# The attention's context product: five bfloat16/float16 products on a block diagonal, or float32 on 32x32 tiles

## The reference, cut to what matters

```
x = x + fake_quant(layernorm(x)) @ fake_quant(ctx)                 # ctx: 16 x 512 x 512
h = layernorm(x)
q, k, v = h @ wq.T + bq, h @ wk.T + bk, h @ wv.T + bv              # reshaped to (token, 32 heads, 16)
scores  = einsum('bshd,bstd->bsht', q, k) / 4                      # heads against heads, for each token
probs   = softmax(scores)
x = x + einsum('bsht,bstd->bshd', probs, v)                        # the context product
x = x + ffn(layernorm(x))     # a router picks 16 of 64 experts of rank 8: z = h @ A.T, times gate, @ B.T
```

## Time and profile before

| | |
|---|---|
| median of 3 runs | 202.35 us (202.15 to 202.36) |
| span of the profiled execution | 198.7 us, 3999 instructions; its own total time is not listed apart from the three runs |
| around the span, against the median | 3.65 us |
| busy: PE / PE weight load / DVE / ACT / POOL | 136.4 / 88.6 / 152.5 / 93.6 / 95.1 us |
| mean granted TensorE clock | 0.887 of 2.4 GHz |
| tiles: q product of tiles 1, 2, 3 starts at | 70.30, 108.81, 144.91 us |

### The profile page before, as it was taken

The page is one execution under the profiler, slowest core; times in us unless marked ns, Lnnn a source line. Parts: engine busy times, 40 slices in busy tenths (PEclk is TensorE's granted clock), DMA queues, the critical chain, the costliest instruction groups (busy, mean ns, idle before and its releaser), DMA issues.

```text
span 198.7 us, 3999 instructions
## 1 busy us (share of the span) xinstructions
PE 136.4 (69%) x1630; PEld 88.6 (45%) x1630; DVE 152.5 (77%) x258; ACT 93.6 (47%) x117; POOL 95.1 (48%) x101
## 2 busy tenths in 40 slices
PE   0012587940904799787957998597799949589884
PEld 0002473410803654336646443393754418585543
DVE  0768579999699657799997679999844999958331
ACT  0289414875892084822693856327016734301120
POOL 2738036668870858753049698313347832201000
PEclk9999999995585579997888999969699996969999
DMA  4999999995738138000000100000010000000101
GB/s 103 422 412 404 398 406 416 372 409 208 269 157 351 76 66 358 3 0 0 3 3 0 52 2 3 0 3 0 3 56 0 0 0 3 0 3 0 54 3 53
DMA packets 7218, 25.20 MB, mean 127 GB/s; under 512 B 1184, under 2 KB 1440, under 8 KB 5280
## 3 DMA queue, kind: packets, MB, share of 16 engines
q1 hardware_dynamic: 7056, 24.94, 32.7%
q10 hardware_dynamic: 144, 0.00, 0.0%
HBM read 23.89 MB, written 1.05 MB: 126 GB/s over the span
## 4 chain that ended last, share of the span: by engine, by line
DVE 53%; PE 17%; issue 12%; POOL 9%; ACT 4%; DMA 2%; POOLq 0%; DVEq 0%; ACTq 0%
PE ps_b L1098 6%; DVE qdiag L756 5%; DVE vdiag L787 4%; DVE vdiag_lo L798 4%; DVE kT L764 4%; DVE qT L743 4%; DVE h L636 3%; POOL q_sb L358 3%; DVE stats L630 3%; DVE probs L636 2%; POOL rstd L343 2%; DMA sc_in<-in_quant_dram 2%; DVE s_max L805 2%; DVE kT_lo L768 2%; DVE vdiag L929 2%
## 5 line engine op out<-in xcount | busy, mean ns | idle before, releaser
L466 ACT ACTIVATE cu<-raw,sc_in,sc_recip 128x2048 uint8<-128x2048 f32 x15 | 30.7, 2085 | 0.8 <-DMA raw<-in_ctx_dram 0.8
L1171 PE MATMUL ps_att<-qT,vdiag 128*128 128x32 f16 x128 | 17.3, 186 | 9.7 <-DVE qT L821 9.7
L352 POOL TENSOR_SCALAR cbf<-cu 128x2048 bf16<-128x2048 uint8 x10 | 19.7, 1974 | 4.8 <-ACT cu L466 4.5
L340 POOL TENSOR_SCALAR var_eps<-mean_var 128x1 f32<-128x1 f32 x12 | 3.6, 301 | 36.0 <-DVE mean_var L632 35.8
L1152 PE MATMUL ps_att<-kT,qdiag 128*128 128x32 bf16 x128 | 10.4, 183 | 14.6 <-DVE kT_lo L768 7.6
L378 POOL TENSOR_TENSOR k_pack<-probs,k_pack 128x512 f16<-128x512 f32 x7 | 9.4, 1351 | 19.0 <-ACT k_pack L535 19.0
L1152 PEld LDWEIGHTS ps_att<-kT,qdiag 128*128 128x128 bf16 x128 | 10.1, 101 | 17.8 <-issue 17.8
L1171 PEld LDWEIGHTS ps_att<-qT,vdiag 128*128 128x128 bf16 x128 | 13.2, 103 | 10.6 <-DVE vdiag_lo L798 10.6
L1172 PE MATMUL ps_att<-qT,vdiag 128*128 128x32 f16 x128 | 17.3, 186 | 0.0
L1173 PE MATMUL ps_att<-qT,vdiag 128*128 128x32 f16 x128 | 17.3, 186 | 0.0
L1174 PE MATMUL ps_att<-qT,vdiag 128*128 128x32 f16 x128 | 17.3, 186 | 0.0
(11 more groups left out here) (141 smaller groups left out, 460.7 us busy)
## 6 DMA issues: line engine op xcount, KB each, us to landing
raw<-in_ctx_dram SPq DMA_DIRECT2D x15, 1024.0 KB, 7.0
raw<-in_ctx_dram SPq DMA_DIRECT2D x2, 512.0 KB, 11.8
wq<-in_L_attn_wq_dram SPq DMA_DIRECT2D x1, 1024.0 KB, 14.1
wk<-in_L_attn_wk_dram SPq DMA_DIRECT2D x1, 1024.0 KB, 10.8
wv<-in_L_attn_wv_dram SPq DMA_DIRECT2D x1, 1024.0 KB, 15.0
wa<-in_L_ffn_A_w_dram SPq DMA_DIRECT2D x1, 1024.0 KB, 18.6
wb<-in_L_ffn_B_w_dram SPq DMA_DIRECT2D x1, 1024.0 KB, 16.1
x_sb<-in_x_dram SPq DMA_DIRECT2D x1, 768.0 KB, 8.6
```

What stands on the lines that cost most here:

```text
L352: nc.gpsimd.tensor_scalar(cbf[:, n % BF_SLOTS, :, :], cu8[:, n % U8_SLOTS, :], -CENTER, 1.0, ALU.add, ALU.mult).then_inc(sem_ctx_bf_pool, 1)
L466: nc.scalar.activation(cu8[:, n % U8_SLOTS, :], raw[:, n % RAW_SLOTS, :], ACT.Identity, bias=sc_in[:, 3:4], scale=sc_recip[:, 2:3]).then_i ...
L1171: nc.tensor.matmul(ps_att[:, i, :], v_hi, e_hi, start=True, stop=False)
```

## The change

The context product takes its two operands as they are, in float32. For each step i PE takes four products, one for each sequence j: the stationary operand is eT (32 partitions of quarter j, 32 columns), the moving one vT (the same partitions, 16 columns and one of ones), and the output 32x17 at the partitions of quarter j. The splitting of v and of the exponentials goes, and with it hi_v, mid_v, the POOL commands for them, place_v, spread_v_lo, both block diagonals with their clearing, and the scaling by 16384. transpose_v takes v_sb and writes vT. transpose_context reads 17 columns a step in place of 32, and oT lies with the channel outside and the head inside. eT, vT, oT, attn, q1 and h1 get buffers of their own, and the waits follow: bias_k waits for k's low part of the tile before in place of x2_ready, bias_v for vT, transpose_q for place_q of the tile before, transpose_probs for the context of the tile before. Scores, order of work, CUT and the filler products stay.

```
@@ buffers @@
-        vdiag = sb("vdiag", [P, Q * P * 2], BF16)
-        vdiag_lo = sb("vdiag_lo", [P, Q * P], BF16)
+        eT = sb("eT", [P, Q, H])
+        vT = sb("vT", [P, Q, HD + 1])
-        e_pack = k_pack[:, :].bitcast(F16)
-        eT = qT[:, :].bitcast(F16)
-        oT = probs
+        oT = sb("oT", [P, HD + 1, H])
-        vT = words(k_sb)
-        attn = k_sb
+        attn = sb("attn", [P, D])
...
@@ gpsimd @@
-            def make_e_lo(t, part):
...
-            nc.gpsimd.memset(words(vdiag_lo), 0).then_inc(sem_v_lo_zeros, 1)
+            nc.gpsimd.memset(vT[:, :, HD:HD + 1], 1.0).then_inc(sem_v_ones, 1)
...
-                take_hi(t + 1, v_sb[:, :], view(v_pack[:, :], 0, [[2, D]]), sem_v_hi, sem_v_rest)
-                make_lo(t + 1, v_sb[:, :], view(v_pack[:, :], 1, [[2, D]]), v_lo[:, :], sem_v_rest, sem_v_mid, sem_v_lo)
-                for part in range(2 if t < TILES - 1 else 1):
-                    make_e_lo(t, part)
...
@@ scalar @@
-            def hi_v(t):
-            def mid_v(t):
...
                 nc.scalar.activation(probs[:, half, :], probs[:, half, :], ACT.Exp,
                                      scale=HD ** -0.5).then_inc(sem_s_exp, 1)
-                act.wait_ge(sem_s_exp, 2 * t + part + 1)
-                act.wait_ge(sem_kT_ready, 2 * (t + 1))
-                nc.scalar.activation(probs[:, half, :], probs[:, half, :], ACT.Copy,
-                                     scale=E_SCALE).then_inc(sem_e_scaled, 1)
-                act.wait_ge(sem_e_scaled, 2 * t + part + 1)
-                nc.scalar.copy(e_pack.rearrange("p (i h w) -> p i h w", h=H, w=2)[:, half, :, 0],
-                               probs[:, half, :]).then_inc(sem_e_hi, 1)
@@ vector @@
             def bias_k(t):
                 if t >= 1:
-                    dve.wait_ge(sem_x2_ready, t)
+                    dve.wait_ge(sem_k_lo, 2 * t)
...
             def transpose_v(t):
-                dve.wait_ge(sem_v_mid, t + 1)
-                dve.wait_ge(sem_k_lo, 2 * (t + 1))
-                nc.vector.transpose(vT.rearrange("p (i d) -> p d i", d=HD),
-                                    words(v_pack).rearrange("p (h d) -> p d h", d=HD)).then_inc(sem_vT_ready, 1)
-            def place_v(t):
-            def spread_v_lo(t):
+                if t == 0:
+                    dve.wait_ge(sem_v_ones, 1)
+                if t >= 1:
+                    dve.wait_ge(sem_context_done, t)
+                dve.wait_ge(sem_v_biased, t + 1)
+                nc.vector.transpose(vT[:, :, 0:HD].rearrange("p i d -> p d i"),
+                                    v_sb[:, :].rearrange("p (h d) -> p d h", d=HD)).then_inc(sem_vT_ready, 1)
...
             def transpose_probs(t, part):
-                nc.vector.transpose(words(qT)[:, values], words(k_pack)[:, values]).then_inc(sem_eT_ready, 1)
+                half = slice(S * part, S * (part + 1))
+                dve.wait_ge(sem_s_exp, 2 * t + part + 1)
+                if t >= 1:
+                    dve.wait_ge(sem_context_done, t)
+                nc.vector.transpose(eT[:, half, :], probs[:, half, :]).then_inc(sem_eT_ready, 1)
...
             def transpose_context(t):
-                nc.vector.transpose(oT[:, :, :], view(ps_att[:, 0, :], 0, [[1, H], [H, Q]])).then_inc(sem_oT_ready, 1)
+                nc.vector.transpose(oT[:, :, :], view(ps_att[:, 0, :], 0, [[1, HD + 1], [H, Q]])).then_inc(sem_oT_ready, 1)
...
-            nc.vector.memset(words(vdiag), 0).then_inc(sem_v_zeros, 1)
...
@@ tensor @@
             def context(t, first, end):
                 if first == 0:
-                    pe.wait_ge(sem_v_diag, 2 * BPT * (t + 1))
-                e_halves = eT.rearrange("p (i h w) -> p i h w", h=H, w=2)
+                    pe.wait_ge(sem_vT_ready, t + 1)
                 for i in range(first, end):
                     if i % S == 0:
                         pe.wait_ge(sem_eT_ready, 2 * t + i // S + 1)
-                    e_hi, e_lo = e_halves[:, i, :, 0], e_halves[:, i, :, 1]
-                    v_hi = view(vdiag[:, :], 2 * P * i, [[2, P]])
-                    v_mid = view(vdiag[:, :], 2 * P * i + 1, [[2, P]])
-                    nc.tensor.matmul(ps_att[:, i, :], v_hi, e_hi, start=True, stop=False)
-                    nc.tensor.matmul(ps_att[:, i, :], v_hi, e_lo, start=False, stop=False)
-                    nc.tensor.matmul(ps_att[:, i, :], v_mid, e_hi, start=False, stop=False)
-                    nc.tensor.matmul(ps_att[:, i, :], v_mid, e_lo, start=False, stop=False)
-                    last = nc.tensor.matmul(ps_att[:, i, :], vdiag_lo[:, P * i:P * (i + 1)], e_hi, start=False,
-                                            stop=True)
+                    for j in range(BPT):
+                        rows = slice(Q * j, Q * (j + 1))
+                        last = nc.tensor.matmul(ps_att[rows, i, 0:HD + 1], eT[rows, i, :], vT[rows, i, :],
+                                                start=True, stop=True)
```

More of the change, by code:

```diff
@@ L250, in build @@
         zgT = sb("zgT", [P, KC, P])
[L252 to L254 removed]
+        q1 = sb("q1", [P, 2, D], BF16)
+        h1 = sb("h1", [P, 2, D])
         ps1 = ps("ps1", [P, 2, 512])
@@ L371, in finish_norm_3 @@
                                         ALU.mult, ALU.mult).then_inc(sem_ln3_shift, 1)
-            def make_e_lo(t, part):
[L375 to L379, removed]
             def residual_2(t):
                 pool.wait_ge(sem_o_recip, t + 1)
-                pool.wait_ge(sem_v_diag, 2 * BPT * (t + 1))
-                nc.gpsimd.tensor_tensor(attn[:, :].rearrange("p (h d) -> p h d", d=HD), oT[:, :, 0:HD],
+                nc.gpsimd.tensor_tensor(attn[:, :].rearrange("p (h d) -> p h d", d=HD),
+                                        oT[:, 0:HD, :].rearrange("p d h -> p h d"),
                                         view(o_recip[:, :], 0, [[1, H], [0, HD]]), ALU.mult).then_inc(sem_o_scaled, 1)
@@ L512, in mid_k @@
                         .then_inc(sem_k_mid, 1)
-            def hi_v(t):
-                act.wait_ge(sem_v_biased, t + 1)
-                if t >= 1:
-                    act.wait_ge(sem_v_diag, 2 * BPT * t)
-                nc.scalar.copy(view(v_pack[:, :], 0, [[2, D]]), v_sb[:, :]).then_inc(sem_v_hi, 1)
-            def mid_v(t):
-                act.wait_ge(sem_v_rest, t + 1)
-                nc.scalar.copy(view(v_pack[:, :], 1, [[2, D]]), v_sb[:, :]).then_inc(sem_v_mid, 1)
             def exp_scores(t, part):
@@ L771, in transpose_v @@
             def transpose_v(t):
-                dve.wait_ge(sem_v_mid, t + 1)
-                dve.wait_ge(sem_k_lo, 2 * (t + 1))
-                nc.vector.transpose(vT.rearrange("p (i d) -> p d i", d=HD),
-                                    words(v_pack).rearrange("p (h d) -> p d h", d=HD)).then_inc(sem_vT_ready, 1)
-            def place_v(t):
-                dve.wait_ge(sem_vT_ready, t + 1)
                 if t == 0:
-                    dve.wait_ge(sem_v_ones, BPT)
+                    dve.wait_ge(sem_v_ones, 1)
                 if t >= 1:
                     dve.wait_ge(sem_context_done, t)
-                for j in range(BPT):
-                    rows = slice(Q * j, Q * j + Q)
-                    nc.vector.tensor_copy(
-                        words(vdiag).rearrange("p (i m) -> p i m", m=P)[rows, :, Q * j:Q * j + HD],
-                        vT.rearrange("p (i d) -> p i d", d=HD)[rows]).then_inc(sem_v_diag, 1)
-            def spread_v_lo(t):
-                if t == 0:
-                    dve.wait_ge(sem_v_lo_zeros, 1)
-                dve.wait_ge(sem_v_lo, t + 1)
-                for j in range(BPT):
-                    rows = slice(Q * j, Q * j + Q)
-                    nc.vector.transpose(
-                        words(vdiag_lo).rearrange("p (i m) -> p m i", m=P // 2)[rows, Q * j // 2:(Q * j + HD) // 2, :],
-                        words(v_lo).rearrange("p (h d) -> p d h", d=HD // 2)[rows]).then_inc(sem_v_diag, 1)
+                dve.wait_ge(sem_v_biased, t + 1)
+                nc.vector.transpose(vT[:, :, 0:HD].rearrange("p i d -> p d i"),
+                                    v_sb[:, :].rearrange("p (h d) -> p d h", d=HD)).then_inc(sem_vT_ready, 1)
             def softmax_shift(t, part):
@@ L928, in _ @@
             copy_q1T(0)
-            nc.vector.memset(words(vdiag), 0).then_inc(sem_v_zeros, 1)
-            dve.wait_ge(sem_v_zeros, 1)
-            for j in range(BPT):
-                nc.vector.memset(view(vdiag[Q * j:Q * j + Q, :], 2 * (Q * j + HD), [[2 * P, Q]]), 1.0)\
-                    .then_inc(sem_v_ones, 1)
             center_ctx(2)
```

42 lines of the change are left out of this document (8 added, 34 removed).

## The result

| | before | after |
|---|---|---|
| median (range, 4 runs each) | 202.25 us (199.48 to 202.36) | 193.3 us (191.53 to 195.1) |
| profiled execution: time, span, mean granted clock | span 198.7, 0.887 | 193.27, span 191.5, 0.902 |
| q product of tiles 1, 2, 3 starts at | 70.30, 108.81, 144.91 | 64.56, 102.18, 137.62 |
| DVE's transpose of the last context product | 178.77 | 170.33 |

The account below looks back on a forecast made before the run. VectorE was taken to bound the kernel (busy 77%, 53% of the last chain). Tiles 0 to 3 gave -1.7 + 3.7 + 5.3 + 4.0 = +11.3; span 198.7 became 210.0, plus 3.65 gave 213.7 us, range 195 to 227.

Parts of the forecast that it names:

- 45 ns a pair: Context products on PE: each pair of weight load and matmul costs 45 ns, with load and stream not overlapping.
- the first rival: Context products on PE: weight loads hidden behind streams, 30 ns a pair, 198.3 us; chance 0.27.
- the rule quoted in the prediction: PE's context products: a weight load overlaps multiplies in flight only where the row group differs.
- my sum of +11.3: Whole kernel: tiles 0 to 3 change by -1.7, +3.7, +5.3 and +4.0 us, together +11.3.
- The second rival: Context products on PE: a token's four matmuls overlap fully, 84 ns a token, DVE's h2 binds, 184 us; chance 0.07.
- Four at a time: Context products on PE: four matmuls of a token run at once, 2.7 us a tile, 184 us; chance 0.07.
- cbf at 17.81: Prologue on DVE: without clearing vdiag, the centring of context 2 starts at 17.6 instead of 18.80.
- The third rival: PE's clock stays low with small tiles: a pair averages 55 ns or more, +21.5, so 224 us; chance 0.25.
- My lower end for a pair: Context products on PE: with the load hidden and only issue spacing counting, a pair costs 26 ns.
- The fourth case: Context products on PE: a token's four matmuls overlap fully and cost one matmul, 84 ns; 184 us, chance 0.07.
- the case without overlap: Context products on PE: loads and streams in sequence, 45 ns a pair (38 to 50), 206 to 219 us; chance 0.37.

Follow-up runs that it names:

- the combined version: Changed kernel with the late context load, four fillers ahead of the last context product, nine between its halves, four and four in tiles 1 and 2's gaps: 185.0 us.

## Why the prediction was wrong

**The step that failed** is "In the new loop every matmul uses another part of the array. With nothing hidden [...] I add 3 for part of that gap and take **45 ns a pair**". Measured: 8.5 ns at the high clock, 13.5 at the low. Two errors in one. The row of the router shows a gap between a product on 16 rows and one on the full array; I read it as a rule for moving between parts. Among four equal tiles it is the reverse: a move to another tile is what lets the work overlap, 26 ns when it never moves for eight tokens, 13.7 with two tiles, 8.5 with four. And even in one tile loads are hidden at the high clock: 26 is about the 27 of the load that the first rival had, not the 42 of load and stream in sequence, so the rule quoted in the prediction, by which such a pair would never overlap, did not hold here. 45 is only seen at the low clock, and that it is my number is chance. (8.5 - 45) ns x 1.02 us a nanosecond is -37 us, which would turn my sum of +11.3 into -26; -7.2 came. The rest was never on the path, since PE then waits. A smaller term failed beside it: I had let the q product of tile 1 run at the high clock, 0.7 us less, and it took 5.69 in place of 4.42.

**The second rival had it**, "Four at a time", with a chance of 0.07: its sign, spacing under 15 ns, and VectorE's h2 as what is late next. Its 184 was 9 us too fast, and here are its steps, measured:

- Tile 0: h2 ready at 60.7, forecast and measured. But q at 64.56, not 62.0: the standstill and the load before it. Without a standstill, in the run with half the steps, q came at 62.35.
- Tiles 1 and 2: from one q product to the next 37.62 and 35.44 us, against 38.51 and 36.10 before, so -0.9 and -0.7. It had -2.2 and -2.3. The q products inside these two stretches, those of tiles 1 and 2, took 5.69 and 5.65 in place of 4.42 and 3.68: 1.3 and 2.0.
- Tile 3: from q to the context transpose -1.15, where it had -4.2. The fillers held the start at 165.36, as I had said, the q product took 5.01 in place of 3.68, and the standstill 2.4.
- Tail: +1.24. The smaller transpose gave 0.50 (1.25 to 0.75; I had 0.6), the scaling of attn rose from 0.69 to 1.02, and the output product began at the low clock.

-5.74 - 0.89 - 0.66 - 1.15 + 1.24 = -7.2, the difference of the spans. That about 184 can be had is shown by the combined version's 185.0.

**The terms that held**: cbf at 17.81 (forecast 17.6), y1's transposes of tile 0 at 54.76 (54.8), h2 at 60.7, the 0.12 us for a change between transposes and context (the last of y1's transposes starts at 94.81, the first context record at 95.01, 0.20 later, where in before the bfloat16 context follows such a transpose after 0.11, at 107.81; that the transpose's row reaches to 95.08 is its way through the array), context records 256 a tile, first context record right behind the last filler, DVE idle ahead of the context transposes (5.98 us in the last tile), POOL's attn off the path (1.34 us, in place of 2.04). The third rival's mechanism, the clock, was real but struck elsewhere: it costs the small tiles 5 ns a record (8.5 to 13.5), at most 1.3 us a tile, and the full float32 q product behind them up to 2.0 us.

**The chances** were drawn too narrow on this one number. My lower end for a pair was 26 ns, "load hidden and only the issue spacing counts", and the measured 8.5 lies far under it: I took the spacing of full-array pairs as a floor for small ones. The fourth case's own price, 84 ns a token, is 10.5 a record, so the text held a price under its own lower end. With no row for four tiles at work, the case without overlap had no right to 0.37 against 0.07.

## What to carry to other kernels

Where a change moves work off the engine that carries the chain, and the new work's price has no row, the price on the old engine is the firm half of the sum: here it put h2 of tile 1 right to 0.1 us, and giving VectorE such work back took the whole gain away. Issue small matmuls so that neighbours fall on different tiles; the order of two loops was worth 16 us. A stream of very short matmuls then has two costs of its own: it runs past its instruction supply, and it ends so soon that PE idles and the next full product runs at the low clock; here fillers cut to the gap's length, between two halves of the stream, covered both; the same fillers made the kernel before slower.

## What the runs showed of the hardware

- In these runs PE went on 2.2 to 3.0 us after an instruction transfer, and it stands still for the part of this time for which its instructions don't last: 2.40, 1.98 and 2.15 us in the last tiles above, where 256 instructions are gone in 1.1 us, 1.68 with two tiles in a row, 1.11 with four and four fillers in the gaps, 0.18 with nine fillers ahead of the boundary. The place moves with the count of instructions exactly: 174, 198, 238, 142, 152.
- An instruction transfer comes late where data transfers fill the DMA engines: 60.01 with the context load in the way (standstill 3.14), 57.86 in a run that began 0.7 later without it (0.68). What makes PE ask for the next block was not found.
- Float32 records of 32 rows, 32 columns and 17 moving columns: 26, 13.7 and 8.5 ns with one, two and four tiles at the high clock; 45, 24 and 13.5 at the low.
- Going over from float32 transposes on the full array to products on 32x32 tiles cost some 0.09 us: 0.20 us from the last transpose's start to the first small record's (94.81 to 95.01), against 0.11 where the full array stays in use (107.70 to 107.81 in before).
- The eight float32 records of 512 columns of a q product took 3.70 us at the high clock (3.68 in before) and 5.65 where most of them ran at the low one.
